# Indirect scatters and gathers of GpSimd in groups of four, each waiting for the landing of the one ahead

## The chip, the cores and the metric

The kernel runs on one core of one Trainium2 chip. The metric is the device time of one execution in microseconds (us), the median of several runs. Times inside an execution are given in us from the start of its span. Engines are named as in the profile: PE (TensorE, matrix products), DVE (VectorE), ACT (ScalarE), POOL (GpSimd) and SP (SyncE, which issues plain DMAs here). Indirect DMAs, whose row addresses come from a table in SBUF, are issued by POOL.

## The reference, cut to what matters

Four residual layers work on 2048 tokens of 128 numbers. Layer 1 is where the change lies. It adds to x a gated delta-rule attention and a mixture of eight experts with top-1 routing; a token whose expert is over capacity falls back to expert 0:

```python
xn = _layernorm(x, axis=-1)
x = x + _L1_attn_ref(xn, ...) + _L1_ffn_ref(xn, ...)
...
final_e = _route(tokens, router_w)
out = jnp.zeros_like(tokens)
for e in range(E):
    h = jax.nn.relu(tokens @ W1[e] + b1[e])
    y = h @ W2[e] + b2[e]
    out = out + jnp.where((final_e == e)[:, None], y, 0.0)
```

Layers 2 and 3 follow, each with a small attention and a gated feed-forward part.

## The kernel before

The tokens lie in 16 tiles (CH = TILES = 16) of 128 rows, four tiles to a block (TPB = 4, NBLK = 4). One function writes layer 0, another layers 1 to 3, in phases; a phase is a block in which every engine runs its own list of instructions in a fixed order and waits on semaphores, and at its end all engines meet. Two phases matter.

Phase l1m prepares the attention and routes the tokens. `E.slot` holds for each token the row that it gets in a buffer sorted by expert. When the slots are known, POOL scatters the 16 tiles of normalised tokens (XNT) into the DRAM tensor `gx`, one indirect DMA a tile (L1442). These are the last instructions of POOL in the phase. At the same time PE, ACT and DVE double a block-triangular inverse in three levels (LEVELS = 3). In each level PE makes four groups of products of L with TD (L1602, 32 matmuls in the profile), ACT copies each group to SBUF (L1735), PE multiplies back (L1609 and L1611, eight matmuls in turn; only L1611 in the last level), and DVE subtracts the results from TD and TT (L1929, L1930). The next level's group q waits for DVE's pair q. After level 2 come the products with KBG (L1618), their eviction by ACT (L1738) and five matmuls that do no work (L56); then the phase ends.

Phase l1s begins on SP with the loads of the sorted rows (L2888 to L2891), which wait until all scatters have landed (L2887). PE, ACT and DVE run the first steps of the recurrence, then experts 1 to 7, then the rest of the recurrence over the 16 chunks. A step passes from PE (L2134, L2137) to ACT (L2485, the copy U) and back to PE (L2148, L2151), and to DVE for the state (L2652, L2657). The experts' results go to the DRAM tensor `gy`. When they are stored, POOL gathers each token's row back into XNT, one indirect DMA a tile (L2046), and adds them to x by block (L2051). DVE adds the attention's output in `arrive` (L2684), which waits for POOL's add, and takes the moments; POOL takes the root, DVE normalises. The order of POOL's list is written out by hand:

```python
pool.wait_ge(E.stored, E.stores)
fetch(0)
fetch(1)
add_rows(0)
add_rows(1)
root(0)
fetch(2)
root(1)
fetch(3)
add_rows(2)
add_rows(3)
```

In the list of DVE, `moments(0)`, `moments(1)` and `moments(2)` stand behind steps 8, 11 and 14 of the recurrence. PE turns the normalised block for layer 2 with L2238, and ACT copies it with L2505.

Of the kernel before, what the change touches and what calls it, by code (L numbers as in the profile page):

```python
# [19 lines left out]
TPB = BLK // P  # L20
# [1190 lines left out]
def layer1_phases(nc, S, W):  # L1211
    with Phase(nc, "l1") as big:
        KVA = big.sb("KVA", [P, CH, KVC])
        E = Experts(nc, S, big)
        col = lambda w: w.rearrange("(p a) -> p a", a=1)
        row = lambda w: w.rearrange("(a p) -> a p", a=1)
        with Phase(nc, "l1at") as att:
# [17 lines left out]
            with Phase(nc, "l1m") as ph:  # L1235
# [72 lines left out]
                with ph.block() as block:  # L1308
# [47 lines left out]
                    def _(pool):  # L1356
# [82 lines left out]
                        pool.wait_ge(slot_ready, 1)  # L1439
                        pool.wait_ge(zero_filled, 16 * ZERO_FILLS)  # L1440
                        for t in range(CH):
                            nc.gpsimd.indirect_dma_start(out=E.gx, out_offset=bass.IndirectOffsetOnAxis(ap=E.slot[:, t:t + 1], axis=0),  # L1442
                                                         in_=S.XNT[:, t, :], in_offset=None).then_inc(E.scattered, 16)

# [490 lines left out]
            with Phase(nc, "l1s") as ph:  # L1935
# [52 lines left out]
                gathered = [ph.sem(f"gathered{b}") for b in range(NBLK)]  # L1988
# [29 lines left out]
                with ph.block() as block:  # L2018
# [23 lines left out]
                    @block.gpsimd  # L2042
                    def _(pool):
                        def fetch(b):
                            for t in range(b * TPB, (b + 1) * TPB):
                                nc.gpsimd.indirect_dma_start(out=S.XNT[:, t, :], out_offset=None, in_=S.gy,  # L2046
                                                             in_offset=bass.IndirectOffsetOnAxis(ap=S.slot[:, t:t + 1], axis=0)).then_inc(gathered[b], 16)
# [30 lines left out]
                        pool.wait_ge(power_made, 1)  # L2078
# [9 lines that stand above are left out]
# [934 lines left out]
```

## Time and profile before

| | |
|---|---|
| median of 3 runs | 653.72 us (650.39 to 653.88) |
| the profiled execution | 653.67 us |
| its span | 651.9 us |
| mean granted TensorE clock | 0.958 of full speed |
| busy: PE, DVE, ACT, POOL | 570.2, 452.0, 385.2, 360.6 us |
| scatters L1442 | 16, median 0.958 us, starts 405.2 to 424.4 |
| gathers L2046 | 16, median 0.944 us, starts 502.6 to 536.2 |
| software DMA queue | 1024 packets, 2.10 MB, 1.1% of 16 engines |

A row of a timeline gives the start, the length, the engine, the line of the kernel, the operation, what is written and read, how many instructions are merged, and in brackets how long the engine was idle before and what is taken to have released it. "issue" is idle time in which the profile shows nothing that the engine waited for; "remote" is a release that the profile can't name. The length of an indirect DMA is the time in which POOL makes it, not the time until the data has landed. In the rows of stretches an engine's entry is its busy us with the number of instructions, and the three last numbers are the granted clock, the busy share of the DMA engines, and GB/s.

### The profile page before, as it was taken

To read this page: it belongs to the slowest core of one execution; us is meant where nothing else is said; L and a number is where in the kernel's file an instruction comes from. 1 tells how busy PE (TensorE), PEld (TensorE's weight loads), DVE (VectorE), ACT (ScalarE), POOL (GpSimd) and SP (SyncE) were. 2 spreads that over 40 slices of the span, in tenths; PEclk is the share of its full clock that TensorE was granted. 3 is DMA by queue.
4 is the path that set the end of the run, shared out by engine and by line. 5 is a ranking of instruction groups with operands and counts; after the bars stand their busy time and mean duration, and the time that the engine had idled before them with its cause. 6 is when DMAs were issued, how large, how long until landed. Compare 5 with 4: busy or idle time off the path is not lost. (4 is left out here: it accounts for less than half of the span.)

```text
span 651.9 us, 10717 instructions
## 1 busy us (share of the span) xinstructions
PE 570.2 (87%) x3813; PEld 460.0 (71%) x3813; DVE 452.0 (69%) x798; ACT 385.2 (59%) x751; POOL 360.6 (55%) x306
## 2 busy tenths in 40 slices
PE   5999978899999999896888897678999678989997
PEld 2444677799899987675657676678788666766676
DVE  6799798999989996992857971233333366657663
ACT  3678799779889784563676854013311133747670
POOL 0578788989889782885606507702901561224530
PEclk9999699899999999999998987869999789999999
DMA  4045132344344512000520006101611110000002
GB/s 127 4 85 86 28 74 82 81 98 105 101 109 109 99 33 73 1 2 9 157 58 2 7 20 152 58 9 31 164 31 49 47 30 4 1 2 1 2 1 65
DMA packets 43230, 35.77 MB, mean 55 GB/s; under 512 B 11895, under 2 KB 32297, under 8 KB 43178
## 3 DMA queue, kind: packets, MB, share of 16 engines
q1 hardware_dynamic: 42154, 32.99, 20.9%
q0 software_dynamic: 1024, 2.10, 1.1%
q8 instruction: 31, 0.51, 0.3%
q14 instruction: 21, 0.17, 0.1%
HBM read 28.98 MB, written 6.09 MB: 54 GB/s over the span
## 5 line engine op out<-in xcount | busy, mean ns | idle before, releaser
L891 DVE TENSOR_TENSOR_SCAN l0s_ring<-l_XM,l0s_ring,bank 128x512 f32<-128x512 f32 x96 | 114.5, 1260 | 5.3 <-ACT l_XM L602 4.4
L602 ACT ACTIVATE l_XM<-l_DT,l_negA 128x512 f32<-128x512 f32 x120 | 79.7, 712 | 10.2 <-DVE l0s_ring L891 10.0
L749 POOL TENSOR_TENSOR l0s_ring<-l0s_ring,l0s_c_rest 128x1024 f32<-128x1024 f32 x32 | 65.8, 2056 | 18.3 <-DVE l0s_ring L891 9.1
L749 POOL TENSOR_TENSOR l0s_ring<-l0s_ring,all_XF 128x1024 f32<-128x1024 f32 x31 | 66.5, 2148 | 7.9 <-DVE l0s_ring L891 5.5
L449 PE MATMUL bank<-all_ident,l0s_ring 128*128 128x128 f32 x512 | 66.4, 274 | 0.0
L449 PEld LDWEIGHTS bank<-all_ident,l0s_ring 128*128 128x128 f32 x512 | 58.5, 142 | 0.0
L2046 POOL DMA_INDIRECT all_XNT<-gy,all_slot x16 | 15.5, 971 | 35.3 <-DMA gy<-l1s_ys 31.0
L418 PE MATMUL bank<-all_ident,all_XNT 128*128 128x128 f32 x256 | 33.8, 274 | 1.0 <-DVE l0s_ring L891 0.7
L332 PE MATMUL bank<-l_XM,l_wins 128*128 128x512 f32 x64 | 31.5, 638 | 0.9 <-ACT l_XM L546 0.9
L1417 POOL TENSOR_TENSOR l1m_prep<-l1at_NWT,l1at_level 128x512 f32<-128x512 f32 x12 | 16.9, 1427 | 25.0 <-issue 22.0
L625 ACT ACTIVATE all_XNT<-all_OUTF,l_wins 128x256 f32<-128x256 f32 x72 | 30.5, 495 | 0.2
L1735 ACT ACTIVATE l_wall<-bank 128x512 f32<-128x512 f32 x12 | 6.9, 597 | 39.8 <-PE bank L1602 39.8
L418 PEld LDWEIGHTS bank<-all_ident,all_XNT 128*128 128x128 f32 x256 | 28.8, 141 | 2.0 <-DVE l0s_ring L891 0.9
L1602 PE MATMUL bank<-l1m_TD,l1m_prep 128*128 128x128 f32 x96 | 17.9, 341 | 13.1 <-issue 6.8
L891 DVE TENSOR_TENSOR_SCAN l0s_ring<-l_XM,bank 128x512 f32<-128x512 f32 x24 | 27.4, 1195 | 2.3 <-ACT l_XM L602 2.3
L1929 DVE TENSOR_TENSOR l1m_TD<-l1m_TD,bank 128x512 f32<-128x512 f32 x8 | 5.5, 688 | 32.7 <-remote 13.1
L1602 PEld LDWEIGHTS bank<-l1m_TD,l1m_prep 128*128 128x128 f32 x96 | 15.8, 247 | 14.9 <-issue 10.9
L2058 POOL TENSOR_TENSOR l1s_xlo<-all_XF,l1s_xhi 128x512 fp32r<-128x512 f32 x7 | 7.7, 1093 | 32.1 <-ACT l1s_xhi L2511 32.1
L332 PEld LDWEIGHTS bank<-l_XM,l_wins 128*128 128x128 f32 x64 | 12.3, 203 | 17.3 <-issue 16.0
L2930 PEld LDWEIGHTS bank<-l_w,l_wall 128*128 128x128 f32 x128 | 17.6, 212 | 9.1 <-issue 5.2
L625 ACT ACTIVATE all_XNT<-l_wraw,l_wins 128x256 f32<-128x256 f32 x56 | 23.7, 494 | 0.2
L2361 PE MATMUL bank<-all_wdT,l1s_work 128*128 128x128 f32 x192 | 22.7, 275 | 0.0
(452 smaller groups left out, 1616.6 us busy)
## 6 DMA issues: line engine op xcount, KB each, us to landing
l0s_c_rest<-bc_rows SPq DMA_DIRECT2D x16, 512.0 KB, 5.0
all_XF<-bc_rows SPq DMA_DIRECT2D x16, 512.0 KB, 4.9
l_wall<-in_L_ffn_W SPq DMA_DIRECT2D x14, 256.0 KB, 4.6
all_X<-in_L_attn_x SPq DMA_DIRECT2D x4, 256.0 KB, 3.8
gx<-l1m_TD SPq DMA_DIRECT2D x1, 1024.0 KB, 5.9
gy<-l1m_TD SPq DMA_DIRECT2D x1, 1024.0 KB, 8.6
out<-all_X SPq DMA_DIRECT2D x4, 256.0 KB, 3.1
gy<-l1s_ys SPq DMA_DIRECT2D x7, 128.0 KB, 1.8
```

Source lines behind the costliest of these rows:

```text
L332: last = nc.tensor.matmul(S.bank[j][:, :], wins[:, k, j * P:(j + 1) * P], XM[:, b * BLK + k:b * BLK + k + BLK], start=(k == 0), stop=(k == ...
L418: last = nc.tensor.transpose(decay(n, j)[:, bass.ts(k, P)], buT[i % 2][:, k, j * P:(j + 1) * P], S.ident[:, :])
L449: last = nc.tensor.matmul(y_of(k, j), hc[n % CRING][:, j, bass.ts(k, P)], S.ident[:, :], start=False, stop=(n % DS == DS - 1 and k % 2 == ...
L602: nc.scalar.activation(dst, DT[:, j, block_of(n)], ACT.Exp, scale=negA[:, j, n % DS:n % DS + 1]).then_inc(decay_ready, 1)
L625: last = nc.scalar.activation(buT[i % 2][:, k, :], dtuT[n // DS % 2][:, k, :], ACT.Identity, scale=bT[:, n // DS * TPB + k, DR + n % DS:DR ...
L749: nc.gpsimd.tensor_tensor(hc[n % CRING][:, :, :], h(n)[:, :, :], wide(c_wide[p % HRING][:, n % 2, :]), ALU.mult).then_inc(hc_ready, 1)
L891: nc.vector.tensor_tensor_scan(h(n)[:, j, :], factor, added, before, ALU.mult, ALU.add).then_inc(h_ready, 1)
L1417: nc.gpsimd.tensor_tensor(LL[:, LEVELS - 1 - l, q, :, :], LT[:, quads(q), :], quad(level[:, l, :]), ALU.mult).then_inc(ll_ready, 1)
L1602: last = nc.tensor.matmul(S.bank[2 * q][:, bass.ts(k, P)], LL[:, LEVELS - 1 - l, q, k, :], TD[:, q * TPB + k, :], start=True, stop=True)
L2046: nc.gpsimd.indirect_dma_start(out=S.XNT[:, t, :], out_offset=None, in_=S.gy, in_offset=bass.IndirectOffsetOnAxis(ap=S.slot[:, t:t + 1], a ...
L2361: last = nc.tensor.matmul(out_bank[:, bass.ts(k, P)], hid[b % 2][:, f, bass.ts(k, P)], wdT[:, f, :], start=(b >= NBLK and f == 0 and k == ...
L2930: last = self.nc.tensor.matmul(out, self.hid[b % 2][:, f, bass.ts(k, P)], self.E.down(0)[:, f, :], start=(f == 0), stop=(f == FE - 1))
```

## The change

Before scatter 4, 8 and 12, POOL waits until all scatters ahead have landed. Before each `fetch(b)` but the first, POOL waits until the four gathers of block b - 1 have landed. Nothing else is changed.

```diff
                         for t in range(CH):
+                            if t and t % TPB == 0:
+                                pool.wait_ge(E.scattered, 16 * t)
                             nc.gpsimd.indirect_dma_start(out=E.gx, out_offset=bass.IndirectOffsetOnAxis(ap=E.slot[:, t:t + 1], axis=0),
                                                          in_=S.XNT[:, t, :], in_offset=None).then_inc(E.scattered, 16)
...
                         def fetch(b):
+                            if b:
+                                pool.wait_ge(gathered[b - 1], 16 * TPB)
                             for t in range(b * TPB, (b + 1) * TPB):
                                 nc.gpsimd.indirect_dma_start(out=S.XNT[:, t, :], out_offset=None, in_=S.gy,
                                                              in_offset=bass.IndirectOffsetOnAxis(ap=S.slot[:, t:t + 1], axis=0)).then_inc(gathered[b], 16)
```

## Rows read from the trace of the kernel before

**Rows 1.** The profile page: head, busy time and share of the span by engine.

```profile
span 651.9 us, 10717 instructions
...
PE 570.2 (87%) x3813; PEld 460.0 (71%) x3813; DVE 452.0 (69%) x798; ACT 385.2 (59%) x751; POOL 360.6 (55%) x306
```

**Rows 2.** Timeline of POOL, 396 to 460 us: start, length, instruction, [idle before <-releaser].

```profile
405.18 1.26 POOL L1442 DMA_INDIRECT gx<-all_XNT,all_slot  x1 [0.19 <-issue]
...
424.40 0.95 POOL L1442 DMA_INDIRECT gx<-all_XNT,all_slot  x1 [0.30 <-issue]
...
452.45 0.20 POOL L2072 MEMSET l1s_ST<- 128x128 f32 x1 [27.10 <-POOLq L63]
```

**Rows 3.** Timeline of PE, 402 to 452 us; x counts instructions merged.

```profile
414.41 1.46 PE L1602 MATMUL bank<-l1m_TD,l1m_prep 128*128 128x128 f32 x9
...
420.95 0.37 PE L1602 MATMUL bank<-l1m_TD,l1m_prep 128*128 128x128 f32 x1 [1.53 <-issue]
...
426.61 0.59 PE L1602 MATMUL bank<-l1m_TD,l1m_prep 128*128 128x128 f32 x2 [1.03 <-issue]
...
429.54 2.04 PE L1602 MATMUL bank<-l1m_TD,l1m_prep 128*128 128x128 f32 x8 [2.33 <-DVE l1at_TT L1930]
...
439.59 3.74 PE L1602 MATMUL bank<-l1m_TD,l1m_prep 128*128 128x128 f32 x32
...
443.16 3.74 PE L1611 MATMUL bank<-l1at_TT,l_wall 128*128 128x128 f32 x32
```

**Rows 4.** Timelines of DVE and of ACT, 402 to 452 us.

```profile
412.43 0.69 DVE L1929 TENSOR_TENSOR l1m_TD<-l1m_TD,bank 128x512 f32<-128x512 f32 x1 [1.89 <-PE bank L1611]
...
428.11 0.69 DVE L1929 TENSOR_TENSOR l1m_TD<-l1m_TD,bank 128x512 f32<-128x512 f32 x1 [7.96 <-remote]
...
428.20 1.57 ACT L1735 ACTIVATE l_wall<-bank 128x512 f32<-128x512 f32 x3 [20.14 <-PE bank L1602]
```

**Rows 5.** DMA traffic, 422 to 432 us, in 40 slices of 0.25 us.

```profile
GB/s 197 66 0 0 0 164 99 0 0 0 147 115 0 0 0 131 131 0 0 0 0 0 0 0 0 0 0 0 0 0 0 0 0 0 0 0 0 0 0 0
```

**Rows 6.** Timeline of POOL, 495 to 562 us.

```profile
502.65 1.05 POOL L2046 DMA_INDIRECT all_XNT<-gy,all_slot  x1 [30.98 <-DMA gy<-l1s_ys]
...
511.50 0.94 POOL L2046 DMA_INDIRECT all_XNT<-gy,all_slot  x1 [0.30 <-issue]
...
512.47 1.27 POOL L2051 TENSOR_TENSOR all_X<-all_X,all_XNT 128x512 f32<-128x512 f32 x1
...
514.05 1.26 POOL L2051 TENSOR_TENSOR all_X<-all_X,all_XNT 128x512 f32<-128x512 f32 x1 [0.32 <-DMA all_XNT<-gy,all_slot]
...
528.14 0.94 POOL L2046 DMA_INDIRECT all_XNT<-gy,all_slot  x1 [0.30 <-issue]
...
532.26 1.10 POOL L2046 DMA_INDIRECT all_XNT<-gy,all_slot  x1 [0.20 <-issue]
...
539.19 1.27 POOL L2051 TENSOR_TENSOR all_X<-all_X,all_XNT 128x512 f32<-128x512 f32 x1 [0.79 <-DMA all_XNT<-gy,all_slot]
```

**Rows 7.** Timelines of PE, ACT and DVE between 498 and 541 us.

```profile
513.78 0.80 PE L2148 MATMUL bank<-l1s_U,l1at_KD 128*128 128x128 f32 x2 [5.22 <-issue]
...
513.45 0.28 ACT L2485 ACTIVATE l1s_U<-bank 128x128 f32<-128x128 f32 x1 [6.11 <-remote]
...
519.15 0.28 ACT L2485 ACTIVATE l1s_U<-bank 128x128 f32<-128x128 f32 x1 [0.96 <-PE bank L2137]
...
520.94 0.28 ACT L2485 ACTIVATE l1s_U<-bank 128x128 f32<-128x128 f32 x1 [0.54 <-PE bank L2137]
...
520.57 0.68 DVE L2684 TENSOR_TENSOR all_X<-all_X,bank 128x512 f32<-128x512 f32 x1
...
528.18 0.60 PE L2238 MATMUL bank<-all_ident,all_XNT 128*128 128x128 f32 x4
...
530.03 0.60 ACT L2505 ACTIVATE all_XF<-bank 128x512 f32<-128x512 f32 x1 [1.92 <-PE bank L2238]
```

**Rows 8.** Stretches: busy time of each engine, granted TensorE clock, DMA share.

```profile
513.40:519.00 5.60, 5.22 (x24) 5.09 (x25) 2.45 (x8) 1.11 (x4) 1.60 (x2) 0.51 0.02 4
```

## The prediction

> **What bounds the kernel now.** I read the page first. The profiled execution took 653.67 us with a span of 651.9, so 1.8 us lie around the span, and it stands 0.05 us under the median of 653.72; the sum is made against 653.67. PE is busy for 87% of the span [rows 1]. So an edit on POOL's DMAs is worth something only where those DMAs meet PE's chain. They run in two places: sixteen scatters of L1442 and sixteen gathers of L2046. I opened the timelines of all engines there.
>
> The scatters. POOL issues them back to back from 405.18 to 425.35 and then idles 27.1 us until the phase ends [rows 2]. So POOL's own lateness costs nothing here: phase l1m is ended by PE, whose last big groups are L1602 at 439.59, L1611 at 443.16 and then L1618. Now look at PE during the scatters [rows 3]. At 414.41 it begins the 32 matmuls of level 1's first products (L1602). The same 32 take 3.57 us in level 2 (439.59 to 443.16). In level 1 they come in crumbs, one or two at a time with 1 to 1.5 us of "issue" between them, though a group of eight contains no wait, and the last eight start only at 429.54. DVE and ACT are worse: DVE reacts to a finished product 1.89 us after its last work at 412.43, then after 7.96 us at 428.11, and ACT has nothing issued for 20.14 us before 428.20, where three finished products are evicted in one go [rows 4]. Both come back within 0.1 us of each other, 2.8 us after POOL's last scatter ended. PE was not waiting for them in its crumbs, and they were not waiting for PE: all three engines are held from some 5 to 10 us after the first scatter.
>
> The data is not what is late: each scatter's packets are one short burst, the last over by 426.25, 0.9 us after its issue [rows 5].
>
> The gathers. Eight run without a pause from 502.65 to 512.44 [rows 6]. PE then stands idle 5.22 us to 513.78 and ACT 6.11 us to 513.45, in the middle of a recurrence in which each only waits for the other [rows 7]; again they come back 1.0 us after POOL's last issue. The two later series are groups of four (528.14 is the last start of one, 532.26 the first of the next). After the first of them ACT begins L2505 at 530.03, though the transposes it needs ended at 528.18 + 0.60 = 528.78: a hold of 1.25 us. After the second I found none. So four in a row cost at most 1.25, eight 5.2, sixteen more than ten. I read this as a hold that starts once about four indirect DMAs have run without a pause and lasts until shortly after the series.
>
> **The change, scatters.** It adds three waits of POOL. What each costs POOL is the landing of the last of four. The trace shows landings for gathers only: the eighth gather's issue ended at 511.50 + 0.94 = 512.44 and the add that needed it started at 514.05 (1.6 us); the sixteenth ended at 537.1 (532.26 + three pitches of 1.3 + 0.94) and its add started at 539.19 (2.05) [rows 6]. The scatter's last burst ended 0.8 to 0.9 us after its issue [rows 5], so 0.9 is a lower bound and 2.05 the upper; I take 2.0 less the gap of 0.30 that stands there anyway, 1.7 each, 5.1 in all. POOL's issues then end near 430.5, the last landing near 432.5. Behind them on POOL nothing is queued in this phase, and SP's L2887 wait for all of them comes after the phase end; the cover is the 27.1 us of idle time. If the phase shrinks by the sum below, the end is at 452.4 - 10.8 = 441.6, still 9 us later. Uncovered, the three waits would cost 5.1.
>
> What it gives back: level 1 and the start of level 2, unheld, are 32 matmuls in 3.57 and 64 (L1609, L1611) in 7.14, so level 2 would start at 414.41 + 10.7 = 425.1 and not at 439.59: 14.5 us were lost. Against it stands what four in a row still hold. Nothing is one end. The other is half of what eight cost, 5.2 / 2 = 2.6. I take the measured 1.25, nearest in kind, for the three groups after the first (the first four are over before the first hold shows): 3.75. Scatters: 14.5 - 3.75 = **10.8 us gained**.
>
> **The change, gathers.** Of its three waits, gathered[1] before fetch(2) has already been waited for by add_rows(1), and gathered[2] before fetch(3) is past as well: its last issue ended at 528.14 + 0.94 = 529.1, + 2.05 is 531.1, and fetch(3) starts at 532.26 behind root(1). Both cost nothing. The one between fetch(0) and fetch(1) is real: behind it stand four gathers, add_rows(0), add_rows(1) and root(0), and DVE's moments(0) (L2684) waits for add_rows(0). The fourth gather ends at 507.4 (502.65 + three pitches of 1.26 + 0.94), lands by 509.5, four more take the 4.7 us they take now: 514.2; the add takes 1.27: 515.5 instead of 513.74. L2684 starts at 520.57 today, because the recurrence before it was held 5.2 us and then ran two steps in 5.70 us (ACT at 513.45 and 519.15) at a granted clock of 0.51 [rows 7, 8], the 1.2 GHz level after PE's idling, where a step takes 1.79 at full clock (519.15 to 520.94): 2.1 us more. Without both it comes at 520.57 - 7.3 = 513.3, with 1.25 for each of two groups at 515.8, just after the rows (515.5). Gathers: 520.57 - 515.8 = **4.8 us gained**. From there the chain of moments, roots and normalisation moves as one.
>
> Sum: 653.67 - 10.8 - 4.8 = **638.1 us**. With no hold left: 14.5 and 520.57 - 515.5 = 5.1, so 634.1. With 2.6 a group: 14.5 - 7.8 = 6.7 and 520.57 - 518.5 = 2.1, so 644.9. Its own range is 634 to 645.
>
> **The rivals.** A: no relief. The hold is a price per indirect DMA, not per unbroken series, so the same thirty-two cost the same, and the pauses only spread it. For it: the data never backs up [rows 5], so a wait for landing relieves no visible queue, and PE's crumbs are spread evenly over the scatters. Against: 1.25 and nothing after two fours, 5.2 after eight. Scatters 0, gathers the added 1.7: 655.4. The Trainium skill states a rule that speaks for this side (SBUF — State Buffer, "Who interferes with whom"): a DMA has ports of its own and never contends with a compute engine. By it the hold would have another cause than the DMAs and only the waits would be left, the time of A. The trace speaks against that cause: ACT and DVE come back right behind both series.
>
> B: slower. The engines stay held until the whole series is over, pauses or not. It decides if the release after four takes longer than the pause; after sixteen it took 2.8 us, more than the 2.05 of a landing. Then each release moves with POOL's end: +5.1 in the scatters, +1.7 in the gathers, 660.5.
>
> C: only the gathers are relieved (release 1.0 us after the end, inside the pause), the scatters not (2.8, outside it): 653.67 - 4.8 = 648.9.
>
> **How the numbers follow.** Forecast 0.62, C 0.12, A 0.18, B 0.08. 0.5% (3.3 us) is about what a measurement of this kernel tells from no change. Faster holds the forecast and C, less a little for a C of half its size: 0.73. Same is A and that remainder: 0.18. Slower is B and an A with longer landings: 0.09. The range takes in the forecast's own, C and A: 634 to 655.5; B is left out.
>
> **What would show it.** Right: POOL's scatters in four groups of four with about 2 us between them, ending near 430.5; PE's 32 matmuls of level 1 in about 4 to 7 us instead of 17; no idle of ACT above some 4 us in that stretch; level 2's L1602 near 429; the phase end near 441.6. In the gathers PE's idle of 5.22 gone, and add_rows(0), not the recurrence, level with DVE's L2684. Wrong: crumbs and long waits that go on through each pause, or that begin with the first scatter of a group (A or B, by whether they end with it); a landing of scatters above 4 us, which would push their end towards the shortened phase; a recurrence that then waits for the later rows; a PE clock that falls elsewhere.

## The result and the profile after

The changed kernel takes 634.43 us (median of 6 runs, 632.63 to 636.7) against 653.90 (6 runs, 650.39 to 654.29) for the kernel before: a ratio of 0.971, interval [0.969, 0.973]. The forecast was 638.1, with a range of 634 to 655.5: the result lies 0.4 us above its lower end. The experiments below add something that no step of the forecast foresaw: on four other chips the kernel before took 632.5 to 633.1 us without any change, and on the one of them where both kernels were timed, the change made it 0.3% slower.

The page of the changed kernel; its profiled execution took 636.67 us, 2.2 above its median (against [rows 1]):

```profile
span 635.0 us, 10717 instructions
...
PE 566.0 (89%) x3813; PEld 456.0 (72%) x3813; DVE 452.7 (71%) x798; ACT 385.8 (61%) x751; POOL 360.9 (57%) x306
```

The timeline of POOL in the scatters (against [rows 2]; the scatter is now L1444):

```profile
406.37 1.25 POOL L1444 DMA_INDIRECT gx<-all_XNT,all_slot  x1 [0.18 <-issue]
...
412.98 0.96 POOL L1444 DMA_INDIRECT gx<-all_XNT,all_slot  x1 [1.56 <-DMA gx<-all_XNT,all_slot]
...
429.35 0.95 POOL L1444 DMA_INDIRECT gx<-all_XNT,all_slot  x1 [0.30 <-issue]
438.41 0.20 POOL L2076 MEMSET l1s_ST<- 128x128 f32 x1 [8.10 <-POOLq L63]
```

The timeline of PE (against [rows 3]):

```profile
414.82 3.74 PE L1604 MATMUL bank<-l1m_TD,l1m_prep 128*128 128x128 f32 x32
418.39 1.06 PE L1611 MATMUL bank<-l_wall,l1at_TT 128*128 128x128 f32 x8
...
425.54 3.74 PE L1604 MATMUL bank<-l1m_TD,l1m_prep 128*128 128x128 f32 x32
429.11 3.74 PE L1613 MATMUL bank<-l1at_TT,l_wall 128*128 128x128 f32 x32
```

The timelines of ACT and DVE (against [rows 4]):

```profile
417.24 0.60 ACT L1737 ACTIVATE l_wall<-bank 128x512 f32<-128x512 f32 x1 [0.73 <-PE bank L1604]
418.71 1.09 ACT L1737 ACTIVATE l_wall<-bank 128x512 f32<-128x512 f32 x2 [0.88 <-PE bank L1604]
...
424.99 0.69 DVE L1931 TENSOR_TENSOR l1m_TD<-l1m_TD,bank 128x512 f32<-128x512 f32 x1 [1.54 <-PE bank L1613]
```

Read level 1 first. Its 32 matmuls are one piece of 3.74 us, and level 2 starts 425.54 - 414.82 = 10.72 us after it; before it was 439.59 - 414.41 = 25.18 [rows 3]. So 14.46 us are gone. ACT and DVE still come a little late (two evictions run as one pair after 0.88, a subtraction after 1.54), but PE does not wait for them. The phase ends 452.45 - 438.41 = 14.04 us earlier [rows 2].

The timelines of POOL, then of ACT and DVE, in the gathers (against [rows 6, 7]; L2050 is the gather, L2688 DVE's add):

```profile
488.80 1.05 POOL L2050 DMA_INDIRECT all_XNT<-gy,all_slot  x1 [31.19 <-DMA gy<-l1s_ys]
...
495.36 0.94 POOL L2050 DMA_INDIRECT all_XNT<-gy,all_slot  x1 [1.75 <-DMA all_XNT<-gy,all_slot]
...
500.05 1.28 POOL L2055 TENSOR_TENSOR all_X<-all_X,all_XNT 128x512 f32<-128x512 f32 x1
```

```profile
493.18 0.28 ACT L2493 ACTIVATE l1s_UT<-bank 128x128 f32<-128x128 f32 x1 [1.78 <-PE bank L2155]
...
501.01 0.28 ACT L2493 ACTIVATE l1s_UT<-bank 128x128 f32<-128x128 f32 x1 [2.45 <-remote]
...
501.44 0.68 DVE L2688 TENSOR_TENSOR all_X<-all_X,bank 128x512 f32<-128x512 f32 x1
...
517.28 3.80 DVE L2712 TENSOR_SCALAR all_XNT<-all_X,l1s_mv,l1s_rstd 128x128 f32<-128x128 f32 x4
```

L2688 comes 12.64 us after the first gather; before it was 520.57 - 502.65 = 17.92. The hold of 5 to 6 us has become 1.78 - 0.69 = 1.1 and 2.45 - 0.69 = 1.8 on ACT (0.69 is its idle time in an undisturbed step). From L2688 to the end of the span 133.56 us pass, before 131.33: 2.2 are lost again, 2.05 of them in one instruction group, the normalisation L2712, which takes 3.80 while POOL adds rows at 518.00 and 519.70, against 1.75 in the same place before (and 1.11 in r1 and r2 below, where no add falls on it). The account of the two spans: 14.04 - 0.19 (the recurrence in between) + 5.28 - 2.23 = 16.9 = 651.9 - 635.0.

### The profile page after: what moved, and what is told of

It reads as the page before. It is cut to its first block and busy times, and to the rows that moved or that the text cites. A ratio compares the mean times of both kernels' runs of the same rounds, so it can differ in the third digit from the quotient of the medians.

```text
span 635.0 us, 10717 instructions
## 1 busy us (share of the span) xinstructions
PE 566.0 (89%) x3813; PEld 456.0 (72%) x3813; DVE 452.7 (71%) x798; ACT 385.8 (61%) x751; POOL 360.9 (57%) x306
## 5 line engine op out<-in xcount | busy, mean ns | idle before, releaser
L2050 POOL DMA_INDIRECT all_XNT<-gy,all_slot x16 | 15.5, 971 | 37.0 <-DMA gy<-l1s_ys 31.2
L1417 POOL TENSOR_TENSOR l1m_prep<-l1at_NWT,l1at_level 128x512 f32<-128x512 f32 x12 | 16.9, 1444 | 23.4 <-issue 20.5
L1046 POOL TENSOR_TENSOR l0f_ha<-l0f_ha,l0f_hc 128x704 f32<-128x704 f32 x8 | 13.4, 1674 | 15.9 <-DVE l0f_hc L1031 15.9
L2721 DVE SCALAR_TENSOR_TENSOR l1s_work<-bank,l_wall 128x512 f32<-128x512 f32 x24 | 15.9, 684 | 8.8 <-ACT l_wall L2521 7.0
L2365 PEld LDWEIGHTS bank<-all_wdT,l1s_work 128*128 128x128 f32 x192 | 22.1, 192 | 0.0
```

Source lines behind the costliest of these rows:

```text
L2365: last = nc.tensor.matmul(out_bank[:, bass.ts(k, P)], hid[b % 2][:, f, bass.ts(k, P)], wdT[:, f, :], start=(b >= NBLK and f == 0 and k == ...
L2721: nc.vector.scalar_tensor_tensor(hid[b % 2][:, f, :], up_bank[n][:, :], QSCALE, sg[n % 2], ALU.mult, ALU.mult).then_inc(hid_done, 1)
```

## Experiments

The theory to test was that an unbroken series of indirect DMAs holds PE, ACT and DVE, and that a pause of POOL, long enough, frees them. Rivals: the landing matters and not the pause; the gain is in the gathers' order; it needs groups as small as four. The first four kernels each take one part of the change, or change one size. All four ran on one chip. In the tables, "before" is the kernel before on the same chip.

**One part alone.** e1_scatter_only has the waits of the scatters and not those of the gathers; e2_gather_only the reverse.

> Only the scatters are grouped, the gathers run as before. My theory (engines are held from about the fifth indirect DMA of an unbroken series until shortly after it, and a pause resets that; the two stretches add up): the phase with the scatters is 14 us shorter as in the changed kernel, the eight gathers hold PE for about 5 us as before, so some 639 to 640 us, 14 under before. Rival (the gain comes only together, or mostly from the gathers' side): less than 8 us under before.

> Only the gathers are grouped, the scatters run unbroken as before. My theory: PE's crumbs and the 14.5 us lost in the scatters are back, the 5.2 us idle in the gathers is gone; about 648 to 649 us, 5 under before. Rival (the wait between the first two fours costs what it frees): within 1.5 us of before.

**Other groups, other pauses.** e3_scatter_eight waits once, after eight scatters. e4_pause_long puts work of POOL in the place of the wait for a landing, about as long (the gap is 1.54 us, with the wait 1.56):

```diff
-                            if t and t % TPB == 0:
+                            if t and t % (2 * TPB) == 0:
                                 pool.wait_ge(E.scattered, 16 * t)
```

```diff
                             if t and t % TPB == 0:
-                                pool.wait_ge(E.scattered, 16 * t)
+                                for i in range(5):
+                                    nc.gpsimd.memset(first[:, :, :], 0.0).then_inc(paused, 1)
+                                    pool.wait_ge(paused, (t // TPB - 1) * 5 + i + 1)
```

> One wait in the scatters, before the ninth, so two series of eight; the gathers as changed. If a hold begins some 5 us after a series begins and ends about 1 us after it, each series of eight holds PE, ACT and DVE for about 5 us as the eight gathers did: the scatter phase loses some 8 to 10 us, so about 643 us. If what counts is only how much was issued on average (one pause of 1.6 us instead of three), the loss is near two thirds of 14.5, about 644, but spread over the whole stretch and not starting late in each series. If any single pause were enough: about 634.

> The three waits for landing in the scatters are replaced by five small memsets of GpSimd in a row into a tile that is no longer read, about 1.5 us of pause without any wait for a DMA. If the pause is what frees the engines: the scatter phase as short as in the changed kernel, about 634 us. Rival (it is the landing, that is the number of DMAs under way, that has to be waited for, or GpSimd being busy that holds the others): some or all of the 14 us come back, 640 to 648 us.

| | us, median | before | ratio [95%] |
|---|---|---|---|
| e1_scatter_only | 632.88 | 632.50 | 0.9999 [0.998, 1.002] |
| e2_gather_only | 634.80 | 632.50 | 1.003 [1.000, 1.006] |
| e3_scatter_eight | 634.70 | 632.50 | 1.004 [1.002, 1.007] |
| e4_pause_long | 634.62 | 632.50 | 1.004 [1.002, 1.007] |

The kernel before takes 632.50 us on this chip, 21.4 less than in the forecast's comparison, so there was no hold to take away. The sixteen unbroken scatters of e2 leave level 2 its 10.72 us behind level 1:

```profile
414.44 3.74 PE L1602 MATMUL bank<-l1m_TD,l1m_prep 128*128 128x128 f32 x32
...
425.16 3.74 PE L1602 MATMUL bank<-l1m_TD,l1m_prep 128*128 128x128 f32 x32
```

e1 and e2 miss their times by 6 us and more. e3 and e4 come within 1 us of one of theirs (634), but only because this chip had nothing to lose: of pause and landing, of four and eight, these runs say nothing. They do say what the waits cost where nothing is gained: the scatters' nothing, the gathers' 0.3%.

**The same two kernels again.** r1_before_again is the kernel before, unchanged, with a profile; r2_after_again the changed one.

> The kernel before, unchanged, timed and profiled once more, because in the last comparison it took 632.5 us and not 653.9. Theory (the hold of PE, ACT and DVE during long series of indirect DMAs is not in the program alone: a chip, or the state it is in, has it or not): the time is near 632.5 or near 654, never between; at 632.5 the profile shows level 1's 32 matmuls of L1602 in 3.6 us and no idle of PE over 2 us in the gathers, at 654 crumbs over 15 us and the idle of 5 us. Rival (the profiled execution of before was a stray one and its hold never cost what I summed): 632.5 with crumbs in the profile.

> The changed kernel once more on the same chip. Theory: without the hold the waits buy nothing, and what they cost shows: in the gathers the landing of the fourth, 1.4 us, if the recurrence then has to wait for the first block's rows (add_rows(0) at 501.3 us against DVE's readiness at about 500), so 1 to 2 us slower than before, 634 us. On a chip with the hold: 634 against 654. Rival (the waits are hidden): the same as before within 0.5 us where no hold shows.

They ran on a second chip of this kind, and both expectations held: r1 633.21 us and r2 634.31, before 632.61; r2's ratio is 1.003 [1.001, 1.005]. Timelines of PE and ACT of r1, and its stretch from 410 to 426 us:

```profile
415.65 3.74 PE L1602 MATMUL bank<-l1m_TD,l1m_prep 128*128 128x128 f32 x32
...
426.37 3.74 PE L1602 MATMUL bank<-l1m_TD,l1m_prep 128*128 128x128 f32 x32
```

```profile
416.75 0.60 ACT L1735 ACTIVATE l_wall<-bank 128x512 f32<-128x512 f32 x1 [7.44 <-PE bank L1602]
417.64 0.60 ACT L1735 ACTIVATE l_wall<-bank 128x512 f32<-128x512 f32 x1 [0.30 <-PE bank L1602]
```

```profile
410.00:426.00 16.00, 16.00 (x146) 16.00 (x145) 8.92 (x14) 2.39 (x4) 12.25 (x13) 1.00 0.18 59
```

The same stretch of the kernel before in the forecast's profile (columns: length, busy us and instructions of PE, PE's loads, DVE, ACT and POOL, granted clock, DMA share, GB/s):

```profile
410.00:426.00 16.00, 9.65 (x63) 8.13 (x63) 3.11 (x5) 0.00 (x0) 11.70 (x13) 0.81 0.15 51
```

This is one program on two chips. In r1 the sixteen scatters run from 407.27 to 427.49, unbroken, at the same 1.26 us from start to start, and no engine notices: level 2 starts 10.72 us after level 1, as in the changed kernel, and ACT evicts every 0.9 us. On the forecast's chip the same scatters leave ACT with no instruction in 16 us and PE with 63 matmuls instead of 146. The account closes: the scatters differ by 25.18 - 10.72 = 14.46, the gathers (first gather to L2684) by 17.92 - 11.23 = 6.69, together 21.15, and the medians by 653.90 - 632.61 = 21.3.

This raises a doubt about the main result: 634.43 us is also what the changed kernel takes here (r2, 634.31). Was it timed where the hold is at all? Its trace says yes. ACT's idle times of 1.78 and 2.45 us in the gathers, and the late evictions of level 1, are in it and not in r2, where ACT idles 0.69 in both of those steps and 0.30 between evictions. This is its row in r2 at the place of the 2.45:

```profile
498.20 0.28 ACT L2493 ACTIVATE l1s_UT<-bank 128x128 f32<-128x128 f32 x1 [0.69 <-PE bank L2155]
```

So in the main comparison both kernels met the hold, and the waits left little of it.

What the change costs on this chip stands in DVE's timelines, r1 first, then r2:

```profile
500.86 0.69 DVE L2684 TENSOR_TENSOR all_X<-all_X,bank 128x512 f32<-128x512 f32 x1 [1.31 <-POOL all_X L2051]
```

```profile
499.75 0.69 DVE L2688 TENSOR_TENSOR all_X<-all_X,bank 128x512 f32<-128x512 f32 x1 [2.79 <-POOL all_X L2055]
```

DVE waits for POOL's first row add in both, and 2.79 - 1.31 = 1.48 us longer in r2: the add stands behind all eight gathers in both, and in r2 behind the wait between them too (L2688 comes 12.73 us after the first gather, L2684 in r1 11.23). The medians of 10 runs each differ by 1.1.

**Another order.** If the row add is what is late, it should stand right behind its own four gathers. e7_add_between and e8_root_early keep all waits; e7 has the order fetch(0), add_rows(0), fetch(1), add_rows(1), root(0), and e8:

```diff
                         fetch(0)
-                        fetch(1)
                         add_rows(0)
-                        add_rows(1)
+                        fetch(1)
                         root(0)
+                        add_rows(1)
```

> The changed kernel with the first block's add put between the two first series of gathers (fetch 0, add 0, fetch 1, add 1, then root 0). Theory: where no engine is held, the price of the grouped gathers is that DVE's moments(0) waits for the first block's rows, 2.8 us in the changed kernel against 1.3 in the one before; with the add in between the rows are there some 5 us earlier and DVE does not wait, so 1.5 to 3 us faster than the changed kernel, 631 to 632.5, level with before or up to 1.3 us under it. On a chip with the hold: 634 or less against 654. Rival (root 0, which now comes after the second add, is late next): 633 to 634.

> As the run above, but root(0) ahead of add_rows(1). Theory: DVE's wait for the rows is gone and the root is not late, so at or below the run above, 630.5 to 632; on a chip with the hold 632 to 634 against 654. Rival (the recurrence paces the stretch and the next wait, for ACT's table load and the first feed-forward unit, takes the gain back): 632.5 or more, the same as before within 0.5 us.

A third chip without the hold: e7 632.75, e8 632.58, before 632.90; ratios 0.9997 [0.998, 1.001] and 0.998 [0.997, 1.000]. L2688 comes 9.85 us after the first gather in both, and DVE no longer waits for POOL there. The 0.3% of the gathers' wait is won back; a gain over the kernel before can't be told, as e8's rival had it.

**The series doubled.** e9_double is the kernel before, with each tile scattered a second time, into `gy`, right behind its first: 32 indirect DMAs without a pause, and SP's wait counts all 32 landings. Those rows are no part of the reference's computation.

```diff
                             nc.gpsimd.indirect_dma_start(out=E.gx, ..., in_=S.XNT[:, t, :], in_offset=None).then_inc(E.scattered, 16)
+                            nc.gpsimd.indirect_dma_start(out=E.gy, ..., in_=S.XNT[:, t, :], in_offset=None).then_inc(E.scattered, 16)
```

> The kernel before with 32 indirect scatters without a pause instead of 16: each tile is also scattered into gy, so the experts' output buffer starts with other contents and the result is not the reference's. It asks whether the chips that show no hold would show one in a longer series. Theory (a hold belongs to the chip or its state, not to the length of a series alone): if before takes near 632.5 on this chip, PE's matmuls of levels 1 and 2 run at full pace through all 32 (32 matmuls of L1602 in 3.6 us), and the phase only ends when the two last levels do or somewhat later, because the scatters now last until about 447 us; the time is some 10 us longer for that alone. Rival (a backlog that grows with every scatter and only reaches the others later): crumbs in PE and long waits in ACT from some point on.

One run of each, on a chip with the hold: 674.07 us against 655.61. Timelines of POOL, PE, ACT and DVE:

```profile
446.05 0.96 POOL L1444 DMA_INDIRECT gy<-all_XNT,all_slot  x1 [0.31 <-issue]
```

```profile
425.13 2.05 PE L1604 MATMUL bank<-l1m_TD,l1m_prep 128*128 128x128 f32 x8 [5.14 <-DVE l1m_TD L1931]
436.25 2.07 PE L1611 MATMUL bank<-l_wall,l1at_TT 128*128 128x128 f32 x8 [9.08 <-issue]
...
441.87 0.37 PE L1613 MATMUL bank<-l1at_TT,l_wall 128*128 128x128 f32 x1 [2.42 <-issue]
```

```profile
435.61 0.60 ACT L1737 ACTIVATE l_wall<-bank 128x512 f32<-128x512 f32 x1 [27.05 <-issue]
451.69 1.57 ACT L1737 ACTIVATE l_wall<-bank 128x512 f32<-128x512 f32 x3 [15.48 <-remote]
```

```profile
452.29 0.69 DVE L1931 TENSOR_TENSOR l1m_TD<-l1m_TD,bank 128x512 f32<-128x512 f32 x1 [27.31 <-PE bank L1613]
```

ACT issues one instruction in 43 us, DVE none in 27, PE single matmuls up to 2.8 us apart. Level 2 starts 460.24 - 414.90 = 45.34 us after level 1. All are free again 4.7 to 5.3 us after the last scatter's end (447.01); after sixteen scatters it was 2.8, after eight gathers 1.0 [rows 2, 4, 6, 7], and 1.7 after the eight gathers of this run. So after the long series the release comes later: 2.8 / 16 = 0.18 and 5.0 / 32 = 0.16 us for each indirect DMA. It isn't a fixed share at the short end: behind the fours of the changed kernel, too, ACT and DVE come back 1.0 us after the last one's end (418.71 against 417.72, 424.99 against 424.01). What a series of 32 does on a chip without the hold, which was the question asked, stays open.

**The order alone.** e10_order_alone is the kernel before with e8's order and no wait of the change.

> The kernel before with only the order of GpSimd's list changed in the second stretch (fetch 0, add 0, fetch 1, root 0, add 1), none of the added waits. Theory: where no engine is held, the waits in the scatters are free and those in the gathers are replaced by the add's own wait, so this equals the run with the waits and the early root, 631.5 to 632.6, and is at most 0.3% under before. If the chip has the hold: the gathers' 5 us are gained and the scatters' 14 are not, 648 to 650 against 654. Rival (the waits in the scatters have a price after all): 1 us or more below the run with the early root.

On a chip with the hold: 650.34 us against 655.63, ratio 0.990 [0.987, 0.994]. Timelines of POOL, DVE and ACT:

```profile
511.00 1.27 POOL L2051 TENSOR_TENSOR all_X<-all_X,all_XNT 128x512 f32<-128x512 f32 x1 [1.69 <-DMA all_XNT<-gy,all_slot]
512.41 0.96 POOL L2046 DMA_INDIRECT all_XNT<-gy,all_slot  x1
```

```profile
428.98 0.69 DVE L1929 TENSOR_TENSOR l1m_TD<-l1m_TD,bank 128x512 f32<-128x512 f32 x1 [10.78 <-remote]
...
515.50 0.68 DVE L2684 TENSOR_TENSOR all_X<-all_X,bank 128x512 f32<-128x512 f32 x1
```

```profile
429.07 1.58 ACT L1735 ACTIVATE l_wall<-bank 128x512 f32<-128x512 f32 x3 [20.90 <-remote]
...
517.49 0.28 ACT L2485 ACTIVATE l1s_U<-bank 128x128 f32<-128x128 f32 x1 [2.21 <-remote]
```

The scatters are held as before (ACT 20.90 us); level 2 starts 441.28 - 414.52 = 26.76 us after level 1 here. In the gathers the row add, which itself waits 1.69 us for the landing, breaks the eight into two fours. L2684 comes 11.01 us after the first gather instead of 17.92, and the kernel is 5.3 us faster. The break does it; the change's own wait isn't needed for it. Whether the break would do it without any wait for a landing, this run doesn't say.

**A shorter pause.** e11_pause_short_order is e10 with two memsets ahead of the fifth, ninth and thirteenth scatter:

```diff
+                            if t and t % TPB == 0:
+                                for i in range(2):
+                                    nc.gpsimd.memset(first[:, :, :], 0.0).then_inc(paused, 1)
+                                    pool.wait_ge(paused, (t // TPB - 1) * 2 + i + 1)
```

> The kernel before with two edits. In the scatters no landing is waited for; ahead of the fifth, ninth and thirteenth stand two short memsets on POOL of about 0.25 us each, so that the gap there is about 0.8 us instead of 0.30 and shorter than the 1.56 us of the wait for a landing. In the gathers, the order alone: a row add between the two groups, and root's adds ahead of the second row add, no wait. If this chip shows the hold (the kernel before near 655): theory 'backlog' (each indirect DMA leaves some 0.15 us of work behind, so a short gap after four of them empties most of it): level 2 starts at most 13 us after level 1 instead of 25, total 636 to 640. Theory 'landing' (what holds the engines is released only when all descriptors are done, so a gap shorter than the landing does not free them): level 2 starts 20 to 27 us after level 1, total 648 to 651 from the gathers alone. If the kernel before is near 632.5 on this chip: level 2 10.7 us after level 1 and a total level with it within 0.3%.

On a third chip with the hold: 644.57 us against 655.71, ratio 0.982 [0.979, 0.985]. Timelines of POOL, PE and DVE:

```profile
413.59 0.48 POOL L1445 MEMSET l1m_first<- 128x128 f32 x2
414.35 0.96 POOL L1447 DMA_INDIRECT gx<-all_XNT,all_slot  x1 [0.28 <-issue]
...
429.16 0.96 POOL L1447 DMA_INDIRECT gx<-all_XNT,all_slot  x1 [0.30 <-issue]
```

```profile
416.87 2.84 PE L1607 MATMUL bank<-l1m_TD,l1m_prep 128*128 128x128 f32 x24
...
435.98 3.74 PE L1607 MATMUL bank<-l1m_TD,l1m_prep 128*128 128x128 f32 x32
```

```profile
421.69 0.69 DVE L1934 TENSOR_TENSOR l1m_TD<-l1m_TD,bank 128x512 f32<-128x512 f32 x1 [3.81 <-remote]
...
431.96 0.69 DVE L1934 TENSOR_TENSOR l1m_TD<-l1m_TD,bank 128x512 f32<-128x512 f32 x1 [8.99 <-remote]
```

Level 2 starts 19.11 us after level 1: just under the 20 to 27 that "landing" expected and well above the 13 of "backlog". A gap of 0.76 us (413.59 to 414.35) that waits for no DMA gives back 25.18 - 19.11 = 6.1 of the 14.5, or 26.76 - 19.11 = 7.7 of 16.0 by e10's trace; each of these traces is one execution on a chip of its own. The gap of 1.56 that ends with a landing gives back all. So a landing is not needed for some relief, and three short gaps are not enough for all of it: the last hold ends 1.84 us after the last scatter's end (430.12), against 2.8 without the gaps. e10's gain in the gathers is there again (11.03 us). The profiled execution took 649.04, 4.5 above the median, but it lost 4.35 of that between the phase's end and the first gather, away from both places.

**The better order with all waits, again.**

> The changed kernel (all its waits) with the gathers in the order fetch, row add, fetch, root's adds, row add. If this chip shows the hold (the kernel before near 655): scatters as in the changed kernel, level 2 starts 10.7 us after level 1, L2688 starts 9.9 to 11 us after the first gather instead of 12.64 with the changed kernel's order and 17.92 before, and DVE's wait for POOL's adds after root is gone; total 630.5 to 634, so 0.965 to 0.969 of before against the changed kernel's 0.9714. Rival: the row add between the groups already waits for the landing, so the remaining holds at the gathers are as in the order alone (1.1 to 2.2 us each on ACT) and take the 2 us back: 634 to 636. If the kernel before is near 632.5 on this chip: 632 to 633.

A fourth chip without the hold: 632.40 us against 633.14, ratio 0.999 [0.997, 1.001]. The row add starts 6.44 us after the first gather, and DVE's add follows it, 9.84 us after that gather, with no wait:

```profile
494.09 1.27 POOL L2055 TENSOR_TENSOR all_X<-all_X,all_XNT 128x512 f32<-128x512 f32 x1 [1.61 <-DMA all_XNT<-gy,all_slot]
```

```profile
497.49 0.68 DVE L2688 TENSOR_TENSOR all_X<-all_X,bank 128x512 f32<-128x512 f32 x1
```

So this version was never timed where the hold is. It is the one to keep: it lost nothing on two chips of the kind on which the change loses 0.3%, and it has every pause that helps on the others. That it would beat the change there is argued from e10, not shown.

## Why the prediction was right, point by point

- **PE, DVE and ACT are held by unbroken series of indirect DMAs.** Right in the forecast's comparison and on the three chips of e9, e10 and e11: lengthening the series makes it worse (e9), breaking it makes it better (e10, e11). The scatters give 14.5 us, the gathers 5.3.
- **Rival A (a price for each indirect DMA).** Out: the sixteen scatters are all there, and level 1 runs as if alone. B (held to the end of the series, whatever the pauses) would show level 2 after 429.35; it starts at 425.54. C would show the scatters still held. The rule of the Trainium skill quoted with A (SBUF — State Buffer, "Who interferes with whom"), that a DMA never contends with a compute engine, would leave nothing to gain. Against it stand the 14.46 us, though no run shows what it is that the engines were held by. On the chips of r1 and e8 the trace agrees with it.
- **"What four in a row still hold", 1.25 for each of three groups: 3.75.** This is the term that was mis-sized. Small holds are there (0.88 and 1.54 us of idle time where r1 has 0.30 and 0.50), but PE has work in hand while ACT and DVE are late, and none reaches it: 0. In the gathers the same 1.25 was about right: 2.5 for two groups, where L2688 comes 12.64 us after the first gather and in r2 DVE stood ready after 9.9. There PE, ACT and DVE wait for each other at every step. Against the median, 638.1 - 634.43 = 3.7, the 3.75 looks like the whole miss, and the text's own figure with "no hold left" was 634.1. That nearness is partly luck. Against the profiled execution the miss is 1.4: 3.2 more gained in the scatters (14.04 for 10.8) and 0.5 in the gathers, less 0.2 in the recurrence and 2.2 behind L2688.
- **The wait costs POOL 1.7.** It costs 1.26 (an idle time of 1.56 instead of 0.30) in the scatters and 1.75 - 0.30 = 1.45 in the gathers. The last scatter ended at 430.30, for 430.5 forecast, and 8.1 us of cover were left, for 9.
- **Gathers 4.8 us.** 5.28. The mechanism was right, and the tie: the row add ends at 501.33, and L2688 starts at 501.44, right behind a recurrence that was held until 501.01. The tie hides what the wait costs: where no recurrence is held, the rows are last, by 1.5 us more (r2).
- **"From there the chain moves as one."** Not quite, in the profiled execution: 2.2 us came back behind it, as told above, and that execution is 2.2 us above the median. Whether the other executions have it isn't known.
- **What was missed.** The forecast took the hold for a property of the program. The program alone doesn't make it: the same kernel has it on some chips and not on others. None of the forecast's rivals had a chip on which the change can only cost. That the main comparison ran where the hold is was luck for the number: on the chip of r1 and r2 the forecast of 15.6 us gained met a loss of 0.3%.

## What to carry to other kernels

When engines in the middle of work stand still with "issue" or "remote" while POOL issues indirect DMAs back to back, break the series into fours with work that POOL has to do anyway, best an add that waits for the rows just fetched; a bare wait does it as well, but puts what stands behind it later. What was shown to free the engines fully in the scatters is a gap of 1.56 us; 0.76 us was too short. Before a stall is explained by the program, profile the same program on a second chip: here it was worth 21 us on some and nothing on others. A wait added against such a stall should be tried on both kinds, and placed where an idle cover of POOL hides it (27.1 us in the scatters), not ahead of what another engine waits for.

## What the runs showed of the hardware

- The same program took 632.5 to 633.1 us on four chips; in the forecast's comparison and on three more chips it took 653.9 to 655.7. There sixteen indirect scatters at 1.26 us each cost the other engines 14.5 us (16.0 on e10's chip), thirty-two made the kernel 18.5 us slower still, and eight gathers held PE and ACT for 5 to 6 us.
- The loss is not the idle time alone: from 414.41 to 439.59 the granted clock of the kernel before was 0.73, a mean of its two levels. After PE's idling, the eight matmuls at 429.54 ran at 0.50 (1.2 GHz) and took 2.04 us, where eight take 1.06 in the changed kernel; in the changed kernel's level 1 it was 1.00 (2.4 GHz).
- With pauses after each four, of 0.30 (none), 0.76 and 1.56 us, the scatters cost 14.5, 8.4 and 0 us. With 4, 8, 16 and 32 in a row the engines were free 1.0, 1.0 to 1.7, 2.8 and 4.7 to 5.3 us after the last. The long series fit a queue that fills a little faster than it empties. The short ones fit something simpler: a release comes 1.0 us after the last of four, so a gap of 1.56 us lets it happen and one of 0.76 doesn't. The profile shows no such queue, and the packets of each scatter are over 0.9 us after its issue [rows 5]. Neither reading is shown.
- What stays open: what the hold is, and whether it is the chip that has it. Each chip was used for one comparison, so a property of the chip and a state that it was in at the time, or something else that ran on it, can't be told apart. Issue times, packets and order of instructions are the same with it and without. Nor were a pause as long as a landing but without one, a series of eight scatters, and e8's version timed on a chip with the hold.
